# Embedding gathers of a wide-and-deep ranker: each gather waits for the table that ends five gathers before it

## The reference

```python
emb = jax.vmap(lambda tab, idx: tab[idx])(tables, cat_features)      # [26, 512, 128]
emb_btd = jnp.transpose(emb, (1, 0, 2))
wide_num = jax.nn.relu(numerical @ w_wide + b_wide)
linear_output = jnp.sum(emb_btd, axis=1) + wide_num                  # [512, 128]
x = jnp.concatenate([numerical, emb_btd.reshape(512, 26 * 128)], axis=1)
x = jax.nn.relu(x @ W1 + b1)                                         # 3341 -> 256
x = jax.nn.relu(x @ W2 + b2)                                         # 256 -> 128
return jax.nn.sigmoid(x @ W3 + b3 + linear_output)
```

## Time and profile before

| | |
|---|---|
| median of 3 runs | 142.0 us (141.84 to 142.08) |
| the profiled execution | 141.84 us |
| its span, first to last instruction | 140.1 us |
| mean granted TensorE clock | 0.976 of full speed |
| PE busy | 102.4 us (73%) |
| POOL busy | 96.4 us (69%), 101 gathers |
| ACT busy | 20.5 us (15%) |
| DVE busy | 5.8 us (4%) |

### The profile page before, as it was taken

How to read it: one execution, slowest core, us unless ns; L and a number is a source line. 1 busy time by engine, 2 the same in 40 slices (tenths; PEclk the granted TensorE clock), 3 DMA queues, 4 the chain that set the end, 5 groups by cost and what they waited for, 6 DMA issues and landing times.

```text
span 140.1 us, 1840 instructions
## 1 busy us (share of the span) xinstructions
PE 102.4 (73%) x386; PEld 59.6 (43%) x386; DVE 5.8 (4%) x22; ACT 20.5 (15%) x42; POOL 96.4 (69%) x108
## 2 busy tenths in 40 slices
PE   0594299965859488568549567939959999788991
PEld 0224265531435144324315332435445655446880
DVE  2400100000000000000000000000000000002221
ACT  0400011110111011011101100101110221113431
POOL 2777877778777777777777777777777777777000
PEclk9999999999999999999999999986977999999999
DMA  3989954532355665562452443442623612223210
GB/s 88 316 283 267 234 93 48 57 61 58 51 53 60 59 42 61 55 62 59 49 68 51 50 59 54 43 73 48 56 61 49 48 55 59 56 48 63 39 42 19
DMA packets 9246, 10.84 MB, mean 77 GB/s; under 512 B 3018, under 2 KB 7619, under 8 KB 9235
## 3 DMA queue, kind: packets, MB, share of 16 engines
q0 software_dynamic: 3232, 6.63, 36.6%
q1 hardware_dynamic: 4624, 3.80, 9.3%
q10 hardware_dynamic: 1379, 0.29, 1.2%
HBM read 10.45 MB, written 0.26 MB: 76 GB/s over the span
## 4 chain that ended last, share of the span: by engine, by line
POOL 61%; issue 20%; PE 10%; DMA 3%; ACT 1%; POOLq 1%; DVE 1%; ACTq 0%
POOL emb L197 61%; PE first_layer L287 4%; PE mlp L299 2%; DMA emb<-in_L_rec_tables,row_idx 2%; DMA first_cat<-in_r_cat_features 2%; PE first_layer L263 1%; PE total L293 1%; ACT late_t L412 1%; POOLq L47 1%; PE turn L278 1%; PE total L258 1%; PE turn L246 0%; PE total L307 0%; ACT y L421 0%; DVE h L373 0%
## 5 line engine op out<-in xcount | busy, mean ns | idle before, releaser
L197 POOL DMA_INDIRECT emb<-in_L_rec_tables,row_idx x100 | 94.3, 943 | 30.5 <-issue 30.5
L263 PE MATMUL first_layer<-emb_t,w 128*128 128x512 f32 x96 | 48.9, 633 | 3.0 <-ACT emb_t L404 2.9
L246 PE MATMUL turn<-ident,emb 128*128 128x128 f32 x96 | 16.5, 298 | 23.4 <-DMA emb<-in_L_rec_tables,row_idx 23.4
L404 ACT COPY emb_t<-turn 128x512 f32<-128x512 f32 x24 | 14.1, 586 | 101.9 <-PE turn L246 88.8
L246 PEld LDWEIGHTS turn<-ident,emb 128*128 128x128 f32 x96 | 11.4, 148 | 40.1 <-DMA emb<-in_L_rec_tables,row_idx 36.9
L258 PE MATMUL total<-emb,ident 128*128 128x256 f32 x96 | 27.4, 412 | 0.0
L263 PEld LDWEIGHTS first_layer<-emb_t,w 128*128 128x128 f32 x96 | 17.8, 203 | 21.3 <-issue 13.5
L258 PEld LDWEIGHTS total<-emb,ident 128*128 128x128 f32 x96 | 18.0, 209 | 1.6
L368 DVE TENSOR_SCALAR h<-first_layer,vec_cols 128x128 f32<-128x128 f32 x4 | 1.4, 350 | 116.9 <-PE first_layer L287 116.9
L287 PE MATMUL first_layer<-late_t,w 128*128 128x128 f32 x32 | 5.4, 292 | 1.2 <-ACT late_t L412 0.8
L287 PEld LDWEIGHTS first_layer<-late_t,w 128*128 128x128 f32 x32 | 4.2, 190 | 2.5 <-ACT late_t L412 2.5
(11 more groups left out here) (35 smaller groups left out, 17.8 us busy)
## 6 DMA issues: line engine op xcount, KB each, us to landing
emb<-in_L_rec_tables SPq DMA_DIRECT2D x256, 0.5 KB
w<-in_L_rec_W SPq DMA_DIRECT2D x2, 1152.0 KB, 12.5
emb<-in_L_rec_tables ACTq DMA_DIRECT2D x128, 0.5 KB
emb<-in_L_rec_tables,row_idx POOLq DMA_INDIRECT x100, 3.7
w<-in_L_rec_W SPq DMA_DIRECT2D x1, 768.0 KB, 5.3
w<-in_L_rec_W SPq DMA_DIRECT2D x1, 256.0 KB, 2.9
out<-y SPq DMA_DIRECT2D x4, 64.0 KB, 1.7
w<-in_L_rec_W ACTq DMA_DIRECT2D x1, 128.0 KB
```

The source lines that it names most:

```text
L197: nc.gpsimd.indirect_dma_start(emb[:, t, c, :], None, rows, bass.IndirectOffsetOnAxis(ap=index, axis=0)).then_inc(landed, 16)
L246: mm = nc.tensor.transpose(turn[step % 2][:, chunk(c)], emb[:, t, c, :], ident[:, :])
L263: mm = nc.tensor.matmul(first_layer[k][:, :], w1[:, t, chunk(k)], emb_t[:, step % SLOTS, :], start=False, stop=False, skip_group_check=True)
L404: nc.scalar.copy(emb_t[:, step % SLOTS, :], turn[step % 2][:, :]).then_inc(copied, 1)
```

## The change

In the gather loop a function `pace(k, landed)` is called before each gather. `ends` lists for each body table except table 0 the number of its last gather, (4, 1), (8, 2), ..., (92, 23). Before gather k, POOL waits for each table whose last gather is number k - AHEAD = k - 5 or earlier and that has not been waited for yet. The waits therefore stand before gathers 9, 13, 17, ..., 89 in the body and before 93 and 97 in the late part: before gather 4t + 5, for all four gathers of table t, t = 1 to 23. Nothing else is changed: the same gathers in the same order, to the same places, with the same semaphores.

```diff
@@ -12,6 +12,7 @@
 P = 128
 LATE = 2
 SLOTS = 4
+AHEAD = 5
 BY_SYNC = [(0, 2), (0, 3)]
 BY_SCALAR = [(0, 1)]
 REGS = 32
@@ -203,10 +204,25 @@
             gp.wait_ge(first_steps, 3)
             gather(0, 0, first_row[:, :], gathered[0])
             gp.wait_ge(rows_ready, 1)
-            for t, c in BODY_TILES[1:]:
+
+            landed = 0
+            last_tile = {t: max(k for k, tile in enumerate(BODY_TILES) if tile[0] == t) for t in ORDER if t != 0}
+            ends = sorted((k, t) for t, k in last_tile.items())
+
+            def pace(k, landed):
+                while landed < len(ends) and ends[landed][0] <= k - AHEAD:
+                    landed += 1
+                    if landed == len(ends) or ends[landed][0] > k - AHEAD:
+                        t = ends[landed - 1][1]
+                        gp.wait_ge(gathered[t], 16 * by_pool(t))
+                return landed
+
+            for k, (t, c) in enumerate(BODY_TILES[1:], start=1):
+                landed = pace(k, landed)
                 gather(t, c, column(t, c), gathered[t])
             for n in range(TILES):
                 c, g = divmod(n, LATE)
+                landed = pace(len(BODY_TILES) + n, landed)
                 gather(BODY + g, c, column(BODY + g, c), late_gathered[n])
 
         @block.tensor
```

## The result

| | before | after |
|---|---|---|
| median | 141.99 us (141.84 to 142.08) | 143.99 us (143.86 to 144.12) |
| profiled execution | 141.84 us | 143.71 us |
| span | 140.1 us | 141.9 us |

The ratio is 1.0142, 95% interval 1.0125 to 1.016. The forecast was 144.0, with a range of 143.0 to 145.3.

A forecast was written before the change was run, and what follows sets the result against it. POOL's issue of gathers up to gather 92 was taken as the bound. Waits of 1.79 (table 1) and 0.28 us (table 5) add 2.07 to 141.84, giving 143.91; with 0.16 for the median 144.07, stated as 144.0, range 143.0 to 145.3.

The forecast's parts named there:

- The bound: POOL's issue of gathers up to gather 92 sets the time, 1.248 us each; PE's busy time does not.
- A met wait is free: A wait on POOL whose landing has already come was taken to cost 0, judged from gather 1.
- Table 1: Wait before gather 9 for gather 4, landing after 7.7 us against a limit of 5.94: 1.79 us late.
- The upper end: For the wait before gather 9: 1.95 us, if the gather is busy 1.10 instead of 0.94 us after waiting.
- Table 2, covered by the first stall: Wait before gather 13 for gather 8: already met, since POOL comes at 21.77 and the landing is at 21.55; 0.
- the lower bound: For the wait before gather 9: 1.55 us, using PE's 0.05 us from landing to start.
- Table 5: Wait before gather 25 for gather 20, landing 0.56 us late: ends 0 and 0.56, half taken, 0.28 us.
- The start-up formula: Estimate for one gather DMA: about 2.0 us plus bytes at 436 GB/s, 2.15 us; by that no wait would hold.
- B: Rival: each wait has its own price even when met, 0.05 us, 1.0 us for 20 waits: 145.1; chance 0.06.
- D: Rival: the wait feeds itself, landings from 25 to 50 us lengthen and six more waits hold: 147; chance 0.04.
- C, the clock: Rival: TensorE's clock falls at the end, adding 1.6 us on table 23: 145.7, or 144.8 just before; chance 0.08.
- A, the landings in time: Rival: gather 4 lands within 5.94 us, no wait holds and the time stays at 142.0; chance 0.06.

The follow-up runs named there:

- ahead4: Kernel after with AHEAD = 4 in place of 5; 145.84 us against 141.93 for the kernel before, ratio 1.0269.
- ahead3: Kernel after with AHEAD = 3 in place of 5; 152.50 us against 141.93 for the kernel before, ratio 1.0711.
- w1_late_no_wait: Kernel before, without waits, with the last two pieces of W1 issued by ACT once table 1 has landed; 141.94 against 141.93 us.
- ahead7_again: Kernel after with AHEAD = 7 in place of 5; 141.94 us against 141.93 for the kernel before, ratio 1.0004.
- not_first_again: Kernel after without the wait for table 1, the others kept; 142.78 us against 141.93 for the kernel before, ratio 1.006.
- from_third_again: Kernel after without the waits for tables 1 and 2, the other 21 kept; 142.21 us against 141.92 for the kernel before.
- first_only: Kernel after with only the wait for table 1; on the slow-fetch chip 248.39 us against 252.72 for the kernel before, elsewhere 143.69 against 141.92.

## Why the prediction was right, and where it was not

**The bound** was read rightly. POOL's issue sets the time: in after, ahead4 and ahead3 the idle time that waits added to POOL (1.83, 3.6 and 11.6 us) is the time added to the profiled execution (1.87, 3.64 and 11.8). PE's table 1 moved by 3.7 us in w1_late_no_wait for nothing.

**A met wait is free**: right (ahead7_again, 1.0004). It was read off a single gap, that before gather 1.

**Table 1** was forecast at 1.79 us and measured 1.83. The landing took 7.8 instead of 7.7 us, and from landing to start it is 9.05 + 7.81 = 16.86 to 17.13, 0.26 to 0.27 us, where gather 0's 0.29 had been taken. The upper end, a gather made longer by having waited, doesn't exist: gather 9 was busy for 0.94 us. The least case of the forecast, a landing after 7.0 us, did not come up for gather 4: in the profiles with W1 loaded early it landed after 7.4 to 8.1 us.

**Table 2, covered by the first stall**: right and shown from both sides, 0 in the full change, 1.0 us in not_first_again. What two waits cost is not the sum of what each costs alone. One step of this part does not hold as worded: with the lower bound POOL comes to the wait at 19.04 + 0.94 + 1.55 = 21.53, which is 0.02 before the landing at 21.55, not after it. The term is nothing all the same, since gather 13 would not start before 21.53 + 0.305 = 21.84 anyway.

**Table 5** was the mis-sized term: 0.28 us, half of 0 and 0.56. In the full change it is 0, since the landing of gather 20 went down to 5.3 us. In from_third_again, where nothing before it had waited, it landed after 6.2 us and cost 0.24. Halving two ends gave a number that no execution shows. The median nevertheless came out at 144.0, because the profiled execution after, 143.71, happens to lie 0.28 below its median, while that of before lies 0.15 below: a part of the agreement is luck.

**The start-up formula.** By the Trainium skill ("DMA: Bandwidth & Descriptors", Anatomy of one DMA — SWDGE (gpsimd) path) the estimate was 2.15 us for one such DMA. The least landing in any of these traces is 2.4 us, near the end of ahead3; gathers 4 and 8 beside the W1 load took 7.0 to 9.2 (5.4 where gather 8 had been held back, in ahead4, and 5.1 in ahead3). The traces come near that estimate late in the run alone, and stay 0.2 us or more above it.

**Rivals.** B and D are refuted above. C, the clock: after shows the same fall, hidden in the body; one row of its windows beside the earlier trace rows, at the lower level of 1.2 GHz, and from 98 us to the last matmul the clock is at full speed.

```profile
96.00:98.00 2.00, 2.00 (x5) 1.37 (x5) 0.00 (x0) 0.52 (x1) 1.70 (x2) 0.52 0.28 77
```

No profile has a fall in the tail, so its price there was not seen. On the chip of slow row fetches a fall does lie on the bounding chain, at table 0, after PE had been idle for 20.38 us: in first_only that table took 222.04 - 217.17 = 4.87 us at the lower level and the next one, after the clock had risen, 225.13 - 222.04 = 3.09 (a row of the windows, then two of PE's timeline):

```profile
219.00:221.00 2.00, 2.00 (x4) 0.88 (x4) 0.00 (x0) 0.00 (x0) 0.00 (x0) 0.50 0.00 0
...
222.04 0.60 PE L263 MATMUL turn<-ident,emb 128*128 128x128 f32 x4
...
225.13 0.60 PE L263 MATMUL turn<-ident,emb 128*128 128x128 f32 x4
```

So the 1.6 us that the forecast put on such a fall is of the right size, here 1.8, and only its place was not met.

A, the landings in time, is what AHEAD = 7 makes true, and the time is then that of before, as it said. What spoke for A was put too well: of the gathers a little later, which were said to land in 3.5 to 5 us, has one at 6.0.

The experiments point to no version that beats the kernel before: a wait on POOL can at best be free. By this account fewer or cheaper gathers on POOL would shorten the run, until SP's row fetches bound it; neither was run.

## What to carry to other kernels

Price an added wait by subtraction: the time from issue to landing of what it waits for, less the time until the waiting engine would have come there anyway. On the engine that bounds the kernel the difference goes to the end whole; where it is negative the wait is free. Look for the worst landing, at the moment of the heaviest other traffic, not for the median: here the median was 3.7 us, the limit 5.94, and one landing of 7.8 us made the whole cost. Once one wait has held, recompute the next ones. A transfer issued before the stall has the length of the stall more to land, which made the wait for table 2 free with AHEAD = 5. With AHEAD = 4 its last gather was issued after the stall, and its wait cost 0.66 us.

## What the runs showed of the hardware

- A gather that waited for a DMA started 0.26 us after the landing (gather 9 of the kernel after), while PE started 0.05 us after it. A wait that was already met added nothing to the 0.305 us between two gathers.
- The busy time of gathers 1 to 100 on POOL, 0.94 us, is the same in every trace with landings from 2.4 to 9.2 us. Only gather 0 took 1.10.
- Gathers of equal size land after different times by what else is being loaded: gather 4 took 4.0 us with 2.3 MB of W1 held back and 7.8 us without.
- On one chip SP took 209 to 215 us to issue the same 256 small DMAs, on the others 101.1 to 103.3. A chain that is hidden on one chip can be the bound on another: 252.7 against 142.0 us for the same kernel.
